# Which engine subtracts: the "rests" of the attention inputs move from GpSimd to VectorE

## The reference, cut to what matters

```python
x = x + _L0_attn_ref(_layernorm(x), ...)   # gated recurrence and feed-forward
x = x + _L0_ffn_ref(_layernorm(x), ...)    # mixture, 2 of 16 experts
x = x + _L1_attn_ref(_layernorm(x), ...)   # attention: "layer 0" of the code below
x = x + _L1_ffn_ref(_layernorm(x), ...)    # attention ("layer 1"), then 2 of 8 experts

q = _rope(proj(Wq, bq)); k = _rope(proj(Wk, bk)); v = proj(Wv, bv)
attn = jax.nn.softmax(jnp.einsum('bhtd,bhsd->bhts', q, k) / scale, axis=-1)
```

## Time and profile before

| | us |
|---|---|
| median of 3 runs | 2451.11 |
| lowest and highest run | 2449.45, 2451.28 |
| the profiled execution: its own time | 2448.63 |
| its span in the trace | 2446.7 |
| VectorE busy, share of the span | 80% |
| ScalarE busy, share of the span | 65% |
| GpSimd busy, share of the span | 23% |

### The profile page before, as it was taken

One profiled execution on the slowest core, in us unless ns is written; L12 is line 12 of the kernel. 1 busy time (PEld: TensorE's weight loads), 2 busy tenths in 40 slices (PEclk: granted clock), 3 DMA queues, 4 the chain that ended last, 5 costly groups with the idle time before them and its releaser, 6 DMA issues. The chain is left out here.

```text
span 2446.7 us, 45763 instructions
## 1 busy us (share of the span) xinstructions
PE 2034.3 (83%) x16982; PEld 949.5 (39%) x16982; DVE 1962.0 (80%) x3145; ACT 1595.6 (65%) x3217; POOL 564.4 (23%) x686
## 2 busy tenths in 40 slices
PE   6999787963599999999998769999999999669910
PEld 5888566751222222222222312222222222359910
DVE  7888646766889999999993779999999997366636
ACT  5555443432339988989898518988989889535610
POOL 2444401767310000000000320000000000216455
PEclk9999987986769999999999769999999999679965
DMA  3000030353610111111100441011111110302211
GB/s 112 1 1 1 1 121 16 98 109 98 193 37 20 34 30 34 24 39 33 30 6 11 134 137 32 21 38 26 33 29 34 25 24 6 117 22 76 68 53 58
DMA packets 94413, 121.18 MB, mean 50 GB/s; under 512 B 23665, under 2 KB 56561, under 8 KB 93937
## 3 DMA queue, kind: packets, MB, share of 16 engines
q1 hardware_dynamic: 73712, 78.92, 11.7%
q0 software_dynamic: 8960, 18.37, 3.2%
q10 hardware_dynamic: 11520, 20.98, 2.7%
HBM read 69.70 MB, written 42.99 MB: 46 GB/s over the span
## 5 line engine op out<-in xcount | busy, mean ns | idle before, releaser
L1603 DVE TENSOR_REDUCE mx<-psum 128x1 f32<-128x1024 f32 x1024 | 1175.0, 1216 | 76.5 <-PE psum L1491 75.5
L1580 ACT ACTIVATE p<-psum 128x512 f32<-128x512 f32 x2048 | 1102.5, 596 | 108.3 <-PE psum L1513 65.4
L1525 PE MATMUL psum<-p,v_ext 128*32 128x256 f32 x8192 | 655.8, 392 | 39.5 <-ACT p L1580 39.3
L1491 PE MATMUL psum<-ks,qs 64*128 64x512 bf16 x2048 | 635.2, 394 | 52.5 <-DVE mx L1603 30.1
L1513 PE MATMUL psum<-qs,ks 64*128 64x512 bf16 x2048 | 630.0, 383 | 1.9 <-ACT p L1580 1.5
L1525 PEld LDWEIGHTS psum<-p,v_ext 128*32 128x32 f32 x8192 | 162.0, 108 | 474.1 <-ACT p L1580 254.8
L1513 PEld LDWEIGHTS psum<-qs,ks 64*128 64x128 bf16 x2048 | 123.6, 93 | 403.6 <-ACT p L1580 367.6
L1393 POOL CAST m_near<-mx 128x16 bf16<-128x16 f32 x128 | 25.1, 196 | 1079.1 <-DVE mx L1603 1075.0
L687 POOL DMA_INDIRECT x_in<-n_rows,token_of x152 | 155.7, 1025 | 258.4 <-POOLq L86 183.3
L743 ACT ACTIVATE hid<-psum,stage 128x128 f32<-128x128 f32 x448 | 132.2, 367 | 127.4 <-PE psum L713 127.4
L1491 PEld LDWEIGHTS psum<-ks,qs 64*128 64x128 bf16 x2048 | 118.7, 94 | 114.7 <-DVE mx L1603 81.4
(11 more groups left out here) (253 smaller groups left out, 2184.7 us busy)
## 6 DMA issues: line engine op xcount, KB each, us to landing
qs<-qk_parts SPq DMA_DIRECT2D x128, 104.0 KB
ks<-qk_parts SPq DMA_DIRECT2D x128, 104.0 KB
qk_parts<-piece__1 ACTq DMA_DIRECT2D x40, 256.0 KB, 3.8
qk_parts<-piece__2 ACTq DMA_DIRECT2D x40, 256.0 KB, 3.2
answers<-y_out SPq DMA_DIRECT2D x152, 64.0 KB, 1.5
ew<-in_moe SPq DMA_DIRECT2D x1, 5136.0 KB, 17.2
ew<-in_moe SPq DMA_DIRECT2D x1, 4624.0 KB, 14.6
n_rows<-n_all SPq DMA_DIRECT2D x8, 512.0 KB, 3.2
```

Of the source, the lines that this page charges most:

```text
L1491: pe.matmul(psum[:, bank, :], a["qs"][r, g % NKF, j % KM, i * P:(i + 1) * P], a["ks"][r, g % NKF, j % KM, k * HALF:(k + 1) * HALF], start= ...
L1525: last = pe.matmul(psum[GR * j:GR * j + VW, O_BANK, q], t["v_ext"][:, b * NT + i, VE * (h0 + j):VE * (h0 + j) + VW], a["p"][:, (GH * s + j ...
L1580: act.activation(a["p"][:, n % NP, :], psum[:, S_BANK + n % NS, :], ACT.Exp, scale=DH ** -0.5)\
L1603: dve.tensor_reduce(a["mx"][:, g % 2, h, j, 0, c:c + 1], psum[:, bank:bank + 2, :].rearrange("p a c -> p (a c)"), AX.X, ALU.max)\
```

## The change

`rested_by_vector(b)` says whether VectorE makes the rests of sequence b. It becomes true for all sequences of both layers. That moves 24 subtractions of 128 x 512: 8 in layer 0 (sequences 2 and 3) and 16 in layer 1. GpSimd keeps its gathers in layer 0 and the last pieces of jobs 0 to 7 in layer 1. Nothing else is edited.

```diff
     def rested_by_vector(b):
-        return layer == 0 and b < 2
+        return True
```

## The result

| | before | after |
|---|---|---|
| median of 10 runs each, us | 2451.20 | 2457.07 |
| lowest and highest | 2449.45, 2453.19 | 2453.13, 2459.30 |
| ratio, 95% interval | | 1.0024 (1.0014 to 1.0033) |
| profiled execution, its own time | 2448.63 | 2453.13 |
| span in the trace | 2446.7 | 2451.3 |

The change costs 5.9 us, with an interval of about 3.4 to 8.1 us. I had forecast 6.4 for the difference and 2457.5 for the time. The sum is right; two of its terms are not, and they had opposite signs. That the figure fits so closely is in part luck.

What follows compares the result with a forecast made beforehand. VectorE was taken to end both input stages, with a barrier behind each. Layer 0's +1.5 us and layer 1's +4.9 made +6.4, which on the median of 2451.11 us gave 2457.5, range 2453.0 to 2462.0.

Steps and rivals of the forecast that it cites:

- layer 0, jobs 8 to 15: Layer 0's moved rests 8 to 15, partly covered by VectorE's waits: +1.5 us, between +1.0 and +2.5.
- layer 0, the barrier: Between VectorE's last pieces and layer 0's attention: the attention is delayed by as much as VectorE, nothing added or returned.
- layer 1, jobs 0 to 7: Layer 1's rests 0 to 7: VectorE late by 1.7 us after jobs 0 to 3, 3.3 after job 7.
- layer 1, jobs 8 to 15: Layer 1's rests 8 to 15: +1.2 us for 10 and 11, +0.4 for 12 and 13, the others hidden.
- layer 1, the barrier: Between VectorE's last pieces and layer 1's attention: the attention is delayed by as much as VectorE, nothing added or returned.
- Who bounds the stages: Both input stages: VectorE ends them, GpSimd isn't the bound, and a delay of VectorE's last rotation delays the attention equally.
- Price and cover of a rest: Both input stages: each rest moved to VectorE costs 0.60 us where bare and nothing inside an existing wait.
- The new waits: Layer 1: rest 0 waits 0.3 to 0.4 us, rest 7 about 0.4; rest 4's falls into a wait for TensorE.
- What GpSimd gives back: Layer 1, jobs 0 to 7: VectorE is held up less by GpSimd, 1.1 us back in jobs 0 to 3, then 0.6.
- The lock: GpSimd's last pieces in layer 1 can still stop VectorE: +4.9 us or above; without a lock +3.5 to +4.5.
- A (all hidden): Both input stages: waits and hold-ups absorb the moved rests, +0.6 us, about 2451.7; chance 0.24 including what lies below the forecast.
- B (waits pile up): Layer 1: rests waiting for ScalarE's first pieces delay the rotations queued behind, about +11 us, 2462; chance 0.08.

Runs made afterwards that it cites:

- tail_rests: The kernel before, with the rests of jobs 14 and 15 in both layers moved to VectorE; ratio 0.9999 (0.9987 to 1.0011).
- wait_rests: The kernel before, with only the rests of jobs 9, 14, 15 (layer 0) and 4, 8, 9, 14, 15 (layer 1) moved to VectorE; ratio 1.0013.
- before_again: The kernel before, unchanged, run and profiled once more as a control; ratio 0.9999 (0.9990 to 1.0008).
- small_last: The changed kernel, with GpSimd's eight last pieces of layer 1 cut from 512 columns to 16; ratio to the kernel before 1.0017.
- l1_only: The kernel before, with all 16 rests of layer 1 moved to VectorE and layer 0 as before; ratio 1.0020 (1.0010 to 1.0030).
- stores_sp: The kernel before, with the stores of first and second pieces issued by SyncE's queue instead of ScalarE's; ratio 0.9979 (0.9962 to 0.9995).
- first_sp: The kernel before, with the stores of the first pieces alone issued by SyncE instead of ScalarE; ratio 0.9986 (0.9977 to 0.9995).

## Why the prediction was right, and where it was not

| step | predicted | measured |
|---|---|---|
| layer 0, jobs 8 to 15 | +1.5 | 31.5 against 30.2 (3 profiles each): +1.3 |
| layer 0, the barrier | 0 | 4.14 against 5.39: -1.25 |
| layer 1, jobs 0 to 7 | +3.3 | 47.6 (2) against 42.8 (3): +4.8 |
| layer 1, jobs 8 to 15 | +1.6 | 31.4 (2) against 29.9 (3): +1.6 |
| layer 1, the barrier | 0 | 4.28 against 4.29 (4.30 in one): 0 |
| sum | +6.4 | +6.4; timed +5.9 (3.4 to 8.1) |

- **Who bounds the stages.** Right in layer 1: the gap behind VectorE's last pair is the same before and after. Wrong in layer 0, where I had put the barrier at nothing and it gave 1.25 us back, and the profile before could have shown it: the earlier trace rows have 4.09 us of waiting ahead of the reduction and the earlier trace rows only 3.00, at the same kind of barrier. I read both as "follows VectorE" and didn't ask why they differ. It was GpSimd's last rest and the 6.01 us behind it.
- **Price and cover of a rest.** 0.60 us for a bare one and nothing inside a wait: right. Jobs 8 to 15 came out within 0.2 us in both layers, the final waits went from 1.78 to about 0.6 as said, and tail_rests and wait_rests show the covered ones free. The wait ahead of the last piece of job 8 in layer 0 didn't shrink by a rest, though, but grew from 0.90 to 1.30: ScalarE's three stores ahead of it took 2.54 us instead of 1.94, and they scatter without an edit too (2.59 in before_again, with a wait of 1.54). The wait of 1.86 in layer 1 shrank to 1.49, but it is 0.79 and 0.80 in the two other profiles of the old layer 1: no single wait can be checked against these lines.
- **The new waits.** Rest 0 waited 0.52 (0.4 predicted), rests 4 and 8 waited inside the wait for TensorE, rest 7 did not wait because rest 6 had been held up; it did in small_last, 0.57.
- **What GpSimd gives back.** This is the term that was mis-sized. I let VectorE have 1.7 us back in jobs 0 to 7 of layer 1 (1.1 and 0.6). GpSimd held it up for 2.7, 2.8 and 2.4 us in the three profiles with the old layer 1 and still for 1.7 and 2.5 in the two with the changed one: in the mean 0.5 came back, all of it in jobs 0 to 3. That is 1.2 us of the 1.5 by which this step is off. The rest of it is within the scatter of the stage's start: `rot` of job 1, ahead of any moved instruction, came 14.0 to 14.6 us after the first statistics where layer 1 was the old one and 14.6 to 14.9 where it was new, and 13.9 to 15.1 over all profiles.
- **The lock.** The Trainium skill, "SBUF — State Buffer", section "SBUF: two separate sides", says that GpSimd and a VectorE instruction with two SBUF inputs hold each other off by an exclusive lock, and small_last agrees: with GpSimd's last pieces cut to 16 columns, no rotation or rest is held up. My "+4.9 or above" with the lock was the side to be on: 6.4 on VectorE's own stretches. What I had wrong is how much less GpSimd holds up once it has fewer instructions. In jobs 0 to 7 the last pieces left cost VectorE 1.7 and 2.5 us, where rests and last pieces together had cost 2.4 to 2.8; that it is so because VectorE now has twice as many instructions to be stopped is my reading, and no run separates it from how they happen to fall.
- **The rivals.** A (all hidden) falls with l1_only. B (waits pile up) did not come true, but what layer 1 has over my +4.9 is of its kind, from the lock and not from waits for first pieces: +6.4 is near the upper end that I gave, +7.
- **The clock.** I had left it out, and it scatters an attention by up to 4.5 us, most of the whole effect, in single executions. Only the median of ten runs made the forecast's figure testable.

## What to carry to other kernels

Before work is moved off an engine that seems idle, look at the gap behind the stage as closely as at the busy time within: two barriers of the same kind with different gaps can mean that a second engine is close behind, as here, and freeing it has a value of its own. Work placed inside a measured wait is free, work placed elsewhere costs its full pitch; but where two engines hold each other up, the price of the pair moved here by 0.9 us with the same instructions in the same order, and one profile can't settle a term of that size. And the better use of an idle engine here was SyncE, not VectorE: what VectorE waited for was ScalarE's issuing of stores, which can be seen as "issue" in ScalarE's waits, and moving it brought more than any place of the subtractions that was tried.

## What the runs showed of the hardware that I hadn't expected

- GpSimd takes 6.01 us from its last 128 x 512 subtraction to its first instruction behind the barrier in layer 0, the same in before, before_again, l1_only, stores_sp and first_sp; an engine with little work can so be the last at a barrier.
- Small instructions are stopped too: a `var` of 128 x 8 took 1.15, 1.00 and 1.02 us instead of 0.17 beside a subtraction of GpSimd.
- The moment at which TensorE's clock rises in the attention of layer 1 differs between executions with the same instructions there: it stays at the upper level from 26 us after the first reduction in one, from 44 in another, 4.5 us of time apart. Why isn't shown.
- SyncE issues a 256 KB store every 0.81 us (24 in 19.37 us); in layer 1 of stores_sp, 24 of them behind a fetch ended 5.6 us after the computation they were to be hidden behind.
